# Four shared context slots, an f32 spill and a re-dealt weight preparation in a two-layer gated cross-attention kernel

## The reference, cut to what matters

```python
# layer A
x = x + tanh(g_xattn[0]) * attend_8_heads(layernorm(ctx), layernorm(x), mask)   # own gamma, beta, Wq, Wk, Wv, Wout
x = x + tanh(g_ffn[0]) * moe_top2_of_8(layernorm(x))                            # 8 experts: w1, w3 (512x256), w2 (256x512)
# layer B
x = x + tanh(g_xattn[1]) * attend_16_heads(layernorm(ctx), layernorm(x), mask)  # other gamma, beta, weights
x = x + tanh(g_ffn[1]) * bit_linear_ffn(layernorm(x))                           # ternary weights, depthwise conv, silu
# keys and values of an attention come from concat(context, latents); latents = the normed x
```

## Time and profile before

| | us |
|---|---|
| runs: median, lowest, highest (3) | 1542.29, 1536.02, 1548.83 |
| profiled execution: span from the first to the last instruction | 1538.1 |
| TensorE matmul busy | 1278.3 (83%) |
| VectorE busy | 1053.8 (69%) |
| ScalarE busy | 979.1 (64%) |
| GpSimd busy | 1107.9 (72%) |

### The profile page before, as it was taken

One profiled execution on the slowest core, in us unless ns is written; L12 is line 12 of the kernel. 1 busy time (PEld: TensorE's weight loads), 2 busy tenths in 40 slices (PEclk: granted clock), 3 DMA queues, 4 the chain that ended last, 5 costly groups with the idle time before them and its releaser, 6 DMA issues.

```text
span 1538.1 us, 45142 instructions
## 1 busy us (share of the span) xinstructions
PE 1278.3 (83%) x16918; PEld 994.2 (65%) x16918; DVE 1053.8 (69%) x2830; ACT 979.1 (64%) x2319; POOL 1107.9 (72%) x1359
## 2 busy tenths in 40 slices
PE   0778787679878989878999999899999999998852
PEld 0556565557667866656887887667676676766642
DVE  4768788977556656665666666777777777877634
ACT  2778787456455666554656566678777777777631
POOL 4768788687557755466777776788878888787653
PEclk9989999879999989989999999999999999999965
DMA  9599997486999954368999997344555444555310
GB/s 314 134 193 235 246 239 174 83 221 188 218 233 252 233 95 97 73 159 171 247 258 231 269 247 181 79 97 98 105 91 94 90 105 94 106 82 91 79 32 6
DMA packets 438329, 239.96 MB, mean 156 GB/s; under 512 B 388848, under 2 KB 420320, under 8 KB 429024
## 3 DMA queue, kind: packets, MB, share of 16 engines
q1 hardware_dynamic: 408216, 178.51, 55.7%
q10 hardware_dynamic: 26824, 51.22, 10.6%
q0 software_dynamic: 3072, 7.34, 1.6%
HBM read 107.78 MB, written 35.50 MB: 93 GB/s over the span
## 4 chain that ended last, share of the span: by engine, by line
PE 39%; ACT 13%; DVE 12%; POOL 11%; issue 9%; DMA 9%; DVEq 3%; SPq 2%; ACTq 1%; POOLq 0%
PE bank_ring L1088 9%; PE bank_ring L1126 6%; PE bank_ring L1074 5%; PE bank_out L1107 5%; DVE scores L1340 4%; DMA expert_up<-experts_up 4%; ACT scores L849 4%; PE bank_x L1187 3%; POOL probs L654 3%; PE bank_scores L1048 3%; ACT probs L856 3%; PE bank_x L1140 3%; DMA probs_turned<-probs 3%; ACT values L876 2%; DMA context<-in_ctx 2%
## 5 line engine op out<-in xcount | busy, mean ns | idle before, releaser
L654 POOL TENSOR_TENSOR probs<-scores,probs 112x487 f16<-112x487 f32 x384 | 425.0, 1123 | 234.2 <-ACT probs L856 229.1
L849 ACT ACTIVATE scores<-scores,score_min 112x487 f32<-112x487 f32 x384 | 265.8, 693 | 121.0 <-DVE score_min L1340 118.2
L1357 DVE SCALAR_TENSOR_TENSOR values<-bank_ring,values 128x512 f16<-128x512 f32 x192 | 132.4, 689 | 216.4 <-ACT values L876 216.3
L1340 DVE CUSTOM_DVE_ANT_0 scores<-bank_scores,mask 112x487 f32<-112x487 f32 x384 | 238.1, 657 | 2.9 <-PE bank_scores L1048 2.9
L856 ACT ACTIVATE probs<-scores 112x487 f16<-112x487 f32 x384 | 214.2, 604 | 24.4 <-DMA probs_turned<-probs 9.0
L1088 PE MATMUL bank_ring<-weights,kv_B 128*128 128x128 f16 x3072 | 198.3, 223 | 1.2 <-DVE keys L1352 1.2
L876 ACT ACTIVATE values<-bank_ring 128x512 f16<-128x512 f32 x192 | 112.9, 588 | 128.9 <-PE bank_out L1107 125.2
L1088 PEld LDWEIGHTS bank_ring<-weights,kv_B 128*128 128x128 f16 x3072 | 187.2, 100 | 10.5 <-DVE keys L1352 2.0
L1107 PE MATMUL bank_out<-values,probs_turned 128*128 128x64 f16 x4608 | 171.9, 195 | 17.7 <-issue 11.4
L1074 PE MATMUL bank_ring<-kv_B,weights 128*128 128x488 f16 x768 | 181.0, 372 | 0.0
L1107 PEld LDWEIGHTS bank_out<-values,probs_turned 128*128 128x128 f16 x4608 | 160.1, 100 | 21.4 <-issue 14.0
(11 more groups left out here) (230 smaller groups left out, 2470.9 us busy)
## 6 DMA issues: line engine op xcount, KB each, us to landing
expert_up<-experts_up SPq DMA_DIRECT2D x43, 1024.0 KB, 5.5
expert_down<-experts_down SPq DMA_DIRECT2D x43, 512.0 KB, 6.6
raw_weights<-in_weights ACTq DMA_DIRECT2D x8, 1536.0 KB, 10.7
experts_up<-expert_up ACTq DMA_DIRECT2D x8, 1024.0 KB, 4.4
raw_weights<-in_weights ACTq DMA_DIRECT2D x6, 1024.0 KB, 8.0
probs_turned<-probs SPq DMA_TRANSPOSE x384
context_turned_B<-kv_B ACTq DMA_DIRECT2D x16, 375.0 KB, 8.7
kv_B<-context_turned_B ACTq DMA_DIRECT2D x16, 375.0 KB, 3.7
```

What stands on the lines that cost most here:

```text
L654: pool.tensor_tensor(PR[:, u % 4, 1, 0:KEYS], S[:, u % 4, 0:KEYS], PR[:, u % 4, 0, 0:KEYS], ALU.subtract).then_inc(probs_split, 1)
L849: act_e.activation(S[:, u % 4, 0:KEYS], S[:, u % 4, 0:KEYS], ACT.Exp, bias=rmin[:, u % 4:u % 4 + 1], scale=-1.0, accum_out=rsum[:, g % 2, ...
L1340: dve.tensor_tensor_reduce(out=S[:, u % 4, 0:KEYS], in0=bS[u % 2][0:TOK, 0:KEYS], in1=mask[:, m, 0:KEYS], scale=1.0, scalar=3.0e38, op0=AL ...
L1357: dve.scalar_tensor_tensor(vN[:, j % 2, 1].rearrange("p t d -> p (t d)"), bank("v", j)[:], 1 / WSCALE, vN[:, j % 2, 0].rearrange("p t d -> ...
```

## The change

- `kv_A` and `kv_B` become one tile `kv` with four slots (`n % 4`), which both layers use; a slot is freed by the value projection of the sequence that used it.
- The turned context is spilled in f32, unscaled, from `rawT` (one buffer). Layer B loads it into `rawT` again and scales and rounds it there: ScalarE at `start_b(n) - 7`, GpSimd at `start_b(n) - 6`.
- VectorE scales the latents while it reads them from PSUM; ScalarE copies them to f16, GpSimd only subtracts. The mask has a semaphore of its own, which VectorE's masking waits for.
- GpSimd applies the normalisation of context and latents (`p_apply`) instead of VectorE. The preparation of a context starts up to two steps earlier (`p_step`).
- Expert chunks go 1.5 a step over 32 steps; raw expert weights land in the part of `weights` that layer B's halves fill later (`braw`). Layer B's raw weights are loaded in steps 37, 39 and 58 and split in steps 53 to 69, the first half-heads first; FFN weights are loaded in steps 58 and 60 into the expert buffer, summed in steps 62 to 65 and quantised in steps 68 to 75.
- The DRAM rows are zeroed from a tile of one row, in 6 pieces in steps 4 to 9 and 5 pieces in steps 57 to 61, after the transposes of the step. The x rows are loaded in two parts, the second in step 0.
- The first four expert loads of a batch stand behind the transposes of their step; the second batch's wait for the FFN and layer B weights. Four scatters a step in the first batch as in the second, so that it begins in step 37.

```diff
+SCATTERS = (4, 4)
+KV_SLOTS = 4
+ZERO_PIECES = tuple(tuple(range(0, t, n)) for t, n in zip(TILES, (3, 5)))
+ZERO_STEPS = (4, 57)
+P_AT = {"load": -14, "norm": -12, "rest": -11, "rstd": -10, "apply": -9, "turn0": -8, "turn1": -7, "lat": -6,
+        "spill": -6, "hi": -5, "lo": -4, "lat_hi": -4, "lat_lo": -3}
+def p_step(n, name):
...
+    lead = (0, 0, 1, 1)[n] if n < 4 else 2
+    return max(4 * n + P_AT[name] - lead, FIRST_STEP + 1)
+L1_STEP = 53
+FFN_SUM_STEP, WSUM_STEP, FFN_STEP = 62, 67, 68
+def expert_chunks(j):
+    i = j - EXPERT_STEP
+    return range(min(3 * i // 2, EXPERTS * MOE_CHUNKS), min((3 * i + 3) // 2, EXPERTS * MOE_CHUNKS)) if i >= 0 else range(0)
+        kv_dram = dram("context_kept", (NSEQ, 128, KB, CTX), F32)
+        braw = W[:, 2 * L0_CHUNKS * CHUNK:2 * RES_CHUNKS * CHUNK].bitcast(F32)
+        kv = sb("kv", [128, KV_SLOTS, KB, 2, 512], F16)
+        aff = late1[:, 512:512 + CTX]
@@ SP @@
-            for b in range(2):
-                rows = xs[b].rearrange("(p t) c -> p (t c)", p=128)
...
+                    if 0 <= j - ZERO_STEPS[b] < len(ZERO_PIECES[b]):
+                        zero_rows(b, j - ZERO_STEPS[b])
+                    if b == 1:
+                        sp.wait_ge(ffn_rounded, 8)
+                        sp.wait_ge(l1_split, L1_CHUNKS)
@@ GpSimd @@
+            def p_apply(n):
+                r = rs["P"]
+                pool.wait_ge(rstd_ready["P"], n + 1)
+                for t in range(CT):
+                    last = pool.tensor_scalar(ctxb[0:CP, n % 2, t, :], ctxb[0:CP, n % 2, t, :],
+                                              mv["P"][0:CP, t, 0:1], r[0:CP, t:t + 1], ALU.subtract, ALU.mult)
+                last.then_inc(ctx_normed, 1)
...
             def split_context(n, kb, layer):
+                if layer == 0:
+                    pool.wait_ge(x1_drained, X1_AT[("p_turn", n, kb)])
+                else:
+                    pool.wait_ge(turned_loaded, 16 * (n + 1))
                 if n == 0 and kb == 0:
                     pool.wait_ge(vectors_loaded, 48)
+                    pool.wait_ge(l0_split, L0_CHUNKS)
...
             def split_latents(layer, n):
+                pool.wait_ge(lat_hi[layer], n + 1)
+                if layer == 0:
+                    pool.tensor_tensor(latq[:, n % 2, :, 1], lata[:, 0], latq[:, n % 2, :, 0], ALU.subtract)
+                pool.tensor_tensor(kv[:, at, :, 1, 0:TOK], lata[:, 1], kv[:, at, :, 0, 0:TOK], ALU.subtract)\
+                    .then_inc(kv_ready[layer], 1)
...
             def gather(n):
-                if n == 0:
-                    pool.wait_ge(l1_split, L1_CHUNKS)
@@ ScalarE @@
             def spill_context(n):
+                act_e.wait_ge(x1_drained, X1_AT[("p_turn", n, 1)])
+                act_e.dma_start(kv_dram[n], rawT[:]).then_inc(spilled, 16)
             def reload_context(n):
...
+                act_e.dma_start(rawT[:], kv_dram[n]).then_inc(turned_loaded, 16)
+                if j == EXPERT_STEP + 36:
...
+                if j in (FFN_SUM_STEP - 4, FFN_SUM_STEP - 2):
...
+            def round_context(layer, n):
+                if slot_used(layer, n) > 0:
+                    act_e.wait_ge(v_ready, slot_used(layer, n))
...
+                act_e.activation(latq[:, n % 2, :, 0], lata[:, 0], ACT.Copy)
+                act_e.activation(kv[:, slot(0, n), :, 0, 0:TOK], lata[:, 1], ACT.Copy).then_inc(lat_hi[0], 1)
@@ VectorE @@
                 if name == "p_turn":
                     if n:
+                        dve.wait_ge(ctx_hi[0], 2 * (n - 1) + kb + 1)
                         dve.wait_ge(ctx_lo[0], 2 * (n - 1) + kb + 1)
-                        dve.wait_ge(ctx_lo[1], 2 * (n - 1) + kb + 1)
+                        dve.wait_ge(spilled, 16 * n)
                     dve.tensor_copy(rawT[:, kb], bX1[:, 0:CTX]).then_inc(x1_drained, 1)
                 elif name in ("p_lat", "b_lat"):
...
+                    for i, c in ((0, V_GLAT), (1, V_GATED)) if layer == 0 else ((1, 8 + V_GLAT),):
+                        for kb in range(KB):
+                            scale, shift = latent_vec(c, kb)
+                            last = dve.tensor_scalar(lata[:, i, kb], bX1[:, TOK * kb:TOK * kb + TOK], scale, shift,
+                                                     ALU.mult, ALU.add)
```

More of the change, by code:

```diff
@@ L995, in _ @@
                 load_weights(j)
+                for n in range(NSEQ):
+                    if j == p_step(n, "spill"):
+                        spill_context(n)
                 for t in late(j - 1):
@@ L1223, in part @@
                     j = task[2]
+                    if n == 0 and j == 0:
+                        pe.wait_ge(ffn_rounded, 8)
                     for i in range(4):
```

392 lines of the change are left out of this document (193 added, 199 removed).

## The result

The changed kernel takes 1574.95 us in the median of four runs (1569.02 to 1583.47); the kernel before, beside it, 1544.63 (1536.02 to 1548.83). The ratio is 1.020, 95% interval 1.015 to 1.025: slower by 2%, where 1512 us and 2% faster were forecast. The profiled execution of after has a span of 1574.8 us against 1538.1.

The account below looks back on a forecast made before the run. Bounds were read by stage: DMA in the expert batches, waits in the start and layer A. Terms -10 - 22 - 3 - 14 + 12 + 0 + 7 = -30 took the 1542.29 us median to 1512, range 1490 to 1527.

Parts of the forecast that it names:

- Of the 26.6 us on transposes I take half, 13: Layer A, steps 0 to 33: fewer expert chunks a step win back 13 us of waiting for transposes, ends 0 and 26.6.
- -22: Layer A, steps 0 to 33: sum of all its terms, -22 us, between -42 and +5.
- -2.6: Layer A: GpSimd's work per sequence falls by 2.6 us, with four normalisations gained at 0.57 us each.
- None of the three is above 82%, so I book nothing for this beyond the waits: Layer A: changed work of ScalarE, VectorE and GpSimd counts for nothing, as none is busy above 82%.
- the 14: Layer A: of TensorE's 20.6 us of waits for the mask, 14 us are won back, ends 0 and 20.6.
- it doesn't do what it says: Start: zeroing was not what made context 2 late, so the 10 us stay: 1522 us, no chance of its own.
- the worse one, -6: Start: context 2 arrives at 30.3 us and VectorE's second four splits follow, -6 us; -10 was taken.
- single f32 buffer: Rival, chance 0.12: VectorE's copy of a turned context waits for the previous sequence's spill, 72 us in all: 1584 us.
- -17 forecast: Steps 34 to 55: -3 us from FFN quantisation leaving, -14 from fewer expert load waits with layer B's weights moved.
- +12 forecast: Steps 56 to 78: layer B splits +8, quantisation +8, moved expert loads -4; +12 us, between -9 and +36.
- -4: Steps 56 to 78: expert loads issued behind the transposes cut the transposes' 8.73 us wait, -4 us.
- The rule weighed in the prediction: GpSimd and VectorE lock each other out of a shared port pair, up to 36 us worse; as a rival 0.06, 1548 us.

Follow-up runs that it names:

- e5: The changed kernel with the four normalisations of a sequence back on VectorE instead of GpSimd: 1550.03 us, ratio 1.004 to the kernel before.
- e7: The changed kernel with ScalarE's burst of expert transfers issued one step earlier, GpSimd still normalising: 1547.15 us, ratio 1.004 to the kernel before.
- c2: The changed kernel with the edits of e5, e7 and e3, and the second expert's raw load two steps later: 1560.13 us, ratio 1.009.
- c1: The changed kernel with the edits of e7 and e3, and the second expert's raw load two steps later: 1535.02 us, ratio 0.994.
- e3: The changed kernel with each batch's first four expert loads put back ahead of that step's transposes on SP's queue: 1558.82 us, ratio 1.008.

## Why the prediction was wrong

**The step that failed** is layer A's "Of the 26.6 us on transposes I take half, 13". It took a quarter less traffic a step for half the waiting. The runs showed more waiting in its place: TensorE's wait for transposes rose from 3.5 to 38.7 us, the line holds 33.5% of 275.0 us of the chain, 92 us, and steps 0 to 33 grew by 21.6 us where the sum had -22. Behind it stand two more errors: normalisation on GpSimd "between 0.435 and 0.672, say 0.57" was priced by the nearest rows of the same engine and measured 1.224, so that GpSimd wins nothing a sequence (3.14 and 1.74 less, 4.90 more) where -2.6 was put; and "None of the three is above 82%, so I book nothing for this beyond the waits". A stage's busy share does not say where in a step the work lies: 5.6 us at a stretch in one step of four (step 9, above) moved that step's transposes onto the burst. e5, e7 and c2 show this cause, with 25 to 28 us; why the raw load's packets then take 4 to 9 us is not shown.

**The waits for the mask** went, all 20.6 us. But the 14 did not come back even without spells: c1's steps 0 to 33 take 248.2 us, 5.2 less than before, and e7's 244.5, 8.9 less. A step is 7.3 us in c1 and 7.2 in e7, where I forecast 6.8 (before 7.5). Other waits of TensorE stand in the mask's place: in c1 11.9 us for `context_turned` and 9.3 for `moe_in_f`, where before had 2.8 and 1.4. Which engine's order makes them is not shown.

**The start**: context 2 is no longer late (21.49 to 6.27), so "it doesn't do what it says" is out; whether by the zeroing alone is not told apart, as the raw expert loads, issued at 27.7 us before and at 36.2 now, also left its stretch. Of the two ends the worse one, -6, was right for the projection (-6.7). Then the *single f32 buffer* rival struck, once and here, with 8.7 us of VectorE's wait: I had put it into all twelve later sequences with a lead of 18.6 us, and there spills land in 3.2 to 7.9. The one with the least lead I did not look at. Its 1584 us lie near the measured time, but by luck: the time came from the transposes. In c1 it shows twice, 5.6 us in all: in the start, and in steps 0 to 33, where sequence 3's spill follows a burst and lands after 12.26 us.

**Steps 34 to 55**: -17 forecast, -16.1 measured, though "expert loads under 8% of its chain" was wrong. The chain of the first batch, after, against the earlier trace rows:

```profile
by line: DMA expert_up<-experts_up 21.0%; PE bank_ring L1189 15.3%; PE bank_ring L1151 8.9%; PE bank_x L1203 8.2%; issue 4.7%; PE bank_out L1170 4.3%; SPq L532 4.0%; PE bank_ring L1137 3.9%; PE bank_scores L1111 2.1%; POOL probs L706 1.9%; 
```

21.0% of 179.6 us are 37.7, where 35.8 were before. The stage got shorter, but not by the wait that I named: the size came out right by luck, and its reason is not shown.

**Steps 56 to 78**: +12 forecast, +8.5. The term inside it for the moved expert loads, -4, had the wrong sign and lay past the stage: step 79 is 9 us longer, and e3 gives them back. I counted the queue that the loads left and not what they share the DMA engines with where they arrive.

**Second batch**: 0 forecast, +11.1; 9.3 of it are steps 79 to 82, the same cause (in e3 the batch takes 244.6 us, 8.2 less). **Layer B**: +7 forecast, +4.9.

**The rule weighed in the prediction**, that GpSimd and VectorE lock each other out: by that rule VectorE's instructions in layer A would be longer. As a whole they are not: 195.6 us for 514 instructions after, 207.1 for 543 before, 0.381 us each, though of different kinds. The 48 remainders of expert chunks, which read two tiles of SBUF, do take longer, 41.7 us in all where they took 36.2, with the median the same (0.68 us) and the longest at 2.37 instead of 1.39. That is 5.5 us and not 36. The rule would have raised the sum by up to 36 us, nearer to the time, for a reason that the trace bears out only in small part. Nearer to what happened is the Trainium skill, page "DMA: Bandwidth & Descriptors", section "Issuing engines are not separate DMA queues": transfers from ScalarE, SP and GpSimd end on the same 16 engines and interleave. The trace agrees as far as that SP's transposes and ScalarE's burst delay each other (a transpose 13.00 us in its issue, a raw load's packet up to 9.3 us). The fall from 360 to 30 GB/s is read from the windows above alone.

## What to carry over

When work moves to an engine with room, ask in which step it lies, what of that step it delays, and which periodic traffic the delayed transfer meets; two periods that become equal (four steps here) let a chance meeting recur round after round. A change that lowers the busy time of the engines it relieves and still loses is looked for in the waits, and the cheapest proof of a phase is to shift the other partner by one step: e7 did it in one line. Price a moved operation by its own operation and operands, not by its neighbour's column count.

## What was not expected of the hardware

GpSimd's subtract-and-multiply takes 1.224 us for 256 columns, its multiply-and-add 0.672 for 375, and VectorE's subtract-and-multiply of the same tile 0.408: per column 4.8, 1.8 and 1.6 ns. The shortest of the 48 takes 1.209, so it is not a wait now and then that makes it long; which of operation, operands or writing in place does is not shown.

In a spell packets of the raw load are begun and hardly move: in after fifteen of them, of 12 KB, take 4.1 to 9.3 us each where 0.46 is the median, while from 136 to 139 us others go through one after another, at 0.46 to 0.47 us each. A burst with it takes 15.7 to 27 us and without it 10 to 15.6. The exact condition stays open: a transpose issued 0.1 to 1.5 us behind the first store was there in all 16 spells of the 17 traces, but 20 bursts with one had no spell; in the three runs that made it on purpose in the kernel before, 2 of 12 had one.
